# A layered graph network on one core: the low parts of x2 and x3 are formed on VectorE instead of GpSimd

## What is computed

```python
x = layernorm(x + L0(x))    # diffusion convolution with the adjacency
x = layernorm(x + L1(x))    # two dense layers with batch norm over all graphs: x2 needs all of them
x = layernorm(x + L2(x))    # two graph convolutions, then LSTMs over windows of 1, 2, 3 and 4 nodes
x = layernorm(x + L3(x))    # 8 Euler steps: h = h + dt*(alph*0.5*(adj@h - h) + h@w_eff - h + x0)
```

## Time and profile before

| what | value |
| --- | --- |
| median of 3 runs | 982.8 us (981.35 to 983.01) |
| the profiled execution | 981.68 us |
| its span | 979.6 us, so 2.1 us lie around the span |
| busy: PE, DVE, ACT, POOL | 915.4, 645.8, 576.6, 314.6 us |
| start stage, steps 0 and 1 | 206 to 424 us of the span |
| five middle steps | 424 to 849 us, 85.1 us each |
| step 7 and tail | 849 to 979.6 us |
| granted TensorE clock | 0.98 over the span, 1.00 in the middle steps |

### The profile page before, as it was taken

How to read it: one execution, slowest core, us unless ns; L and a number is a source line. 1 busy time by engine, 2 the same in 40 slices (tenths; PEclk the granted TensorE clock), 3 DMA queues, 4 the chain that set the end, 5 groups by cost and what they waited for, 6 DMA issues and landing times.

```text
span 979.6 us, 14819 instructions
## 1 busy us (share of the span) xinstructions
PE 915.4 (93%) x5115; PEld 792.3 (81%) x5115; DVE 645.8 (66%) x1576; ACT 576.6 (59%) x1292; POOL 314.6 (32%) x527
## 2 busy tenths in 40 slices
PE   8799998968899979999999999999999999999996
PEld 6688886346788658998998898899899889978986
DVE  5889995863467755666667666665766666675644
ACT  5467666823464556557737855774685576467352
POOL 2766555411101242035216304421620442150120
PEclk9999999989799989999999999999999999999999
DMA  5321201301011010101100110120011001000100
GB/s 177 119 75 57 74 33 46 122 27 65 0 33 55 1 33 1 54 2 44 56 11 11 33 66 1 44 65 1 12 33 66 1 22 44 1 12 1 33 22 22
DMA packets 26596, 38.56 MB, mean 39 GB/s; under 512 B 3333, under 2 KB 12422, under 8 KB 26010
## 3 DMA queue, kind: packets, MB, share of 16 engines
q1 hardware_dynamic: 26088, 36.05, 11.1%
q10 hardware_dynamic: 434, 1.57, 0.4%
HBM read 21.89 MB, written 15.73 MB: 38 GB/s over the span
## 4 chain that ended last, share of the span: by engine, by line
PE 55%; DVE 9%; POOL 7%; ACT 6%; issue 3%; ACTq 0%; POOLq 0%; DVEq 0%
PE psum L140 16%; PE psum L142 15%; PE psum L141 15%; PE psum L1811 2%; PE psum L1812 2%; PE psum L1815 2%; ACT gate L1378 1%; ACT x L1409 1%; POOL x_rstd L1311 1%; ACT raw L1474 1%; POOL out_rstd L1311 1%; POOL node_l L1329 1%; PE psum L1986 1%; DVE in_h L1543 1%; DVE shared L1617 1%
## 5 line engine op out<-in xcount | busy, mean ns | idle before, releaser
L1378 ACT ACTIVATE gate<-psum,gate_bias 128x256 f32<-128x256 f32 (+2 forms) x296 | 144.1, 559 | 85.2 <-PE psum L1815 62.4
L140 PE MATMUL psum<-in_h,wih_h 128*128 128x256 f32 (+2 forms) x312 | 107.3, 344 | 11.2 <-DVE in_l L1547 7.9
L142 PE MATMUL psum<-in_h,wih_l 128*128 128x256 f32 (+2 forms) x312 | 104.1, 334 | 0.0
L141 PE MATMUL psum<-in_l,wih_h 128*128 128x256 f32 (+2 forms) x312 | 103.6, 332 | 0.0
L1528 DVE TENSOR_TENSOR gate<-gate 128x256 f32<-128x256 f32 (+2 forms) x48 | 23.9, 499 | 88.9 <-ACT gate L1378 88.8
L140 PEld LDWEIGHTS psum<-in_h,wih_h 128*128 128x128 f32 x312 | 59.2, 190 | 22.9 <-DVE in_l L1547 11.6
L1345 POOL TENSOR_TENSOR gate<-in_h,in_l 128x512 f32<-128x512 f32 x14 | 17.9, 1303 | 164.7 <-DVE in_l L1547 164.7
L140 PE MATMUL psum<-e_h,shared 128*128 128x384 f32 x180 | 62.0, 345 | 5.5 <-DVE shared L1617 3.2
L1381 ACT ACTIVATE gate<-cell 128x512 f32<-128x512 f32 (+2 forms) x80 | 40.3, 503 | 42.6 <-DVE cell L1531 35.4
L141 PEld LDWEIGHTS psum<-in_l,wih_h 128*128 128x128 f32 x312 | 59.4, 190 | 5.1 <-issue 0.2
L142 PEld LDWEIGHTS psum<-in_h,wih_l 128*128 128x128 f32 x312 | 59.4, 190 | 4.7
(11 more groups left out here) (398 smaller groups left out, 2940.4 us busy)
## 6 DMA issues: line engine op xcount, KB each, us to landing
x_spill<-x SPq DMA_DIRECT2D x30, 256.0 KB, 2.0
xt<-in_x_t_dram SPq DMA_DIRECT2D x16, 256.0 KB, 2.7
raw<-x_spill SPq DMA_DIRECT2D x16, 256.0 KB, 3.0
o_spill<-xt SPq DMA_DIRECT2D x14, 256.0 KB, 2.0
xt<-o_spill SPq DMA_DIRECT2D x14, 256.0 KB, 3.2
x<-x_spill SPq DMA_DIRECT2D x14, 256.0 KB, 3.4
out_dram<-raw SPq DMA_DIRECT2D x14, 256.0 KB, 2.3
raw<-in_adj_t_dram ACTq DMA_DIRECT2D x1, 1024.0 KB, 8.8
```

What stands on the lines that cost most here:

```text
L140: pe.matmul(dst, lh, rh, start=start, stop=False, **kw)
L141: pe.matmul(dst, lh, rl, start=False, stop=False, **kw)
L142: return pe.matmul(dst, ll, rh, start=False, stop=stop, **kw)
L1378: nc.scalar.activation(gate[q][:, 0:n], banks[GATE_BANK[q]][:, 0:n], ACT.Tanh if q == 2 else ACT.Sigmoid, bias=gate_bias[:, p - 1, q:q + 1 ...
```

## The change

In all steps but the tail, POOL's pieces `norm` and `x3split` go away and DVE does the same subtraction: a new piece `x2low`, and the piece `x3low` that only the tail had. Each moved instruction is the same operation on the same 128x512 operands. 16 low parts of x2 and 14 of x3 move. ACT, PE and SP keep their order. Where the pieces stand in DVE's lists:

```diff
-        FILL_DVE = [[], ["ysum_1", "ysum_0", "turn_0"], ["x3t_0", "x3sum_1", "outsum"], ["power1_0", "power2_0", "gather0_0"],
-                    ["coefs0_0", "weight0_0"], ["turn_1", "coefs1_0"], ["gather1_0", "x3t_1"], ["power1_1", "weight1_0", "power2_1"],
+        FILL_DVE = [[], ["ysum_1", "ysum_0", "x3low_0", "turn_0"], ["x3t_0", "x3sum_1", "outsum", "x2low_0"], ["power1_0", "power2_0", "gather0_0"],
+                    ["coefs0_0", "weight0_0"], ["turn_1", "coefs1_0", "x3low_1"], ["gather1_0", "x3t_1", "x2low_1"], ["power1_1", "weight1_0", "power2_1"],
...
-        START_DVE = ["turn_0", "columns", "turn_1", "weff", "first_0", "first_1", "gather0_0", "gather0_1", "weight0_0", "weight0_1",
+        START_DVE = ["turn_0", "columns", "turn_1", "weff", "first_0", "x2low_0", "first_1", "x2low_1", "gather0_0", "gather0_1", "weight0_0", "weight0_1",
...
-        ONCE_DVE = [[], ["square", "twice", "turn_0"], ["first_3"], ["gather0_0", "cube", "second_0"],
-                    ["weight0_0", "fourth"], ["turn_1", "second_1", "fc_0"], ["gather1_0", "fc_1", "second_2"],
+        ONCE_DVE = [[], ["square", "twice", "turn_0"], ["first_3", "x2low_0"], ["gather0_0", "cube", "second_0"],
+                    ["weight0_0", "fourth"], ["turn_1", "second_1", "fc_0"], ["gather1_0", "fc_1", "second_2", "x2low_1"],
...
-        NEXT_DVE = [["addlate"], ["x3sum_0", "lift", "turn_0", "turn_vec"], ["mix_3", "x3sum_1", "mix_4"],
+        NEXT_DVE = [["addlate"], ["x3sum_0", "lift", "turn_0", "turn_vec"], ["x3low_0", "mix_3", "x3sum_1", "x2low_0", "mix_4"],
...
-                    ["lift_last", "weight0_0"], ["bias", "coefs0_0", "coefs1_0", "turn_1"]] + FILL_DVE[6:]
+                    ["lift_last", "weight0_0"], ["bias", "coefs0_0", "coefs1_0", "x3low_1", "turn_1"]] + FILL_DVE[6:]
...
-            def norm(g, j):
-                n = GB * g + j
-                pool.wait_ge(x2_hi, n + 1)
-                high, low = nodes(n)
-                nc.gpsimd.tensor_tensor(low[:], x2[j], f32(high[:]), ALU.subtract).then_inc(x2_lo, 1)
...
+            def x2low(g, j):
+                n = GB * g + j
+                dve.wait_ge(x2_hi, n + 1)
+                high, low = nodes(n)
+                nc.vector.tensor_tensor(low[:], x2[j], f32(high[:]), ALU.subtract).then_inc(x2_lo, 1)
```

More of the change, by code:

```diff
@@ L1146, in second_half @@
                     "coefs1", "inner", "innersum", "innerlow", "hlate", "addlate")
-        FRONT_NAMES = ("prep", "turn", "norm", "gather0", "gather1", "weight0", "weight1", "input")
+        FRONT_NAMES = ("x2low", "prep", "turn", "norm", "gather0", "gather1", "weight0", "weight1", "input")
         AHEAD_NAMES = ("ahead",)
@@ L1323, in turn @@
                 (power_of if g == 0 else root)(x2_norm[j], x2_asked, x2_shift, GB * g + j + 1)
-            def norm(g, j):
-                n = GB * g + j
-                pool.wait_ge(x2_hi, n + 1)
-                high, low = nodes(n)
-                nc.gpsimd.tensor_tensor(low[:], x2[j], f32(high[:]), ALU.subtract).then_inc(x2_lo, 1)
             def x3sum(g, j):
                 (power_of if g == G - 1 else root)(x3_norm[j], x3_asked, x3_shift, GB * g + j + 1)
-            def x3split(g, j):
-                n = GB * g + j
-                pool.wait_ge(x3_hi, n + 1)
-                high, low = x3_parts(g, j)
-                nc.gpsimd.tensor_tensor(low[:], x3[:, j, :, :], f32(high[:]), ALU.subtract).then_inc(x3_lo, 1)
             def whole_h(g):
@@ L1360, in split_e @@
                 nc.gpsimd.tensor_tensor(e_l[:], e[:], f32(e_h[:]), ALU.subtract).then_inc(constants_ready, 1)
-            run(None, {"split_e": split_e, "turn": turn, "norm": norm, "x3sum": x3sum, "x3first": lambda g: x3sum(g, 0), "x3early": x3sum, "x3split": x3split, "outsum": outsum,
+            run(None, {"split_e": split_e, "turn": turn, "x3sum": x3sum, "x3first": lambda g: x3sum(g, 0), "x3early": x3sum, "outsum": outsum,
                        "whole": whole_h, "clear": clear}, START_POOL, ONCE_POOL, NEXT_POOL, FILL_POOL, LAST_POOL, TAIL_POOL)
@@ L1778, in _ @@
                             "turn": turn, "weight0": weight0, "weight1": weight1, "x3sum": x3sum, "x3first": lambda g: x3sum(g, 0), "x3early": x3sum, "x3add": x3add,
-                            "addlate": x3add, "x3low": x3low, "outhalf": out_half,
+                            "addlate": x3add, "x2low": x2low, "x3low": x3low, "outhalf": out_half,
                             "x3t": x3t, "innersum": inner_sum, "innerlow": inner_low, "ysum": ysum, "outsum": outsum,
```

## The result

The changed kernel takes 975.51 us (median; 974.51 to 976.4) against 981.35 of the kernel before beside it: ratio 0.9937, 95% interval 0.9922 to 0.9953. Run twice more on other occasions it was at 977.51 (0.9961, 0.9945 to 0.9976) and 976.39 (0.9961, 0.9945 to 0.9976). So it is faster by 3.7 to 5.8 us. The prediction had 981.6, at least 979.6, and is wrong. Its forecast is measured from 982.8, the median of another occasion; the kernel before takes 980.3 to 981.5 in all the comparisons here.

A forecast was written before the change was run, and what follows sets the result against it. PE was taken to bound the kernel, busy 83.93 of 85.08 us in a middle step. Start -0.6, step 0 -0.4, step 1 +0.3 and middle steps -0.5 made -1.2 us, median 982.8 to 981.6, range 979.6 to 983.7.

The forecast's parts named there:

- Step 7 and tail ... 0: Step 7 has nothing behind x3low_0 and no node_l ahead of POOL's root, the tail is unchanged: 0.
- -0.1 a step, -0.5 in five: Middle steps: later turn_0 against earlier root of the last norm; five steps -0.5 us, bounds -2.0 and +1.0.
- D: Middle step: delay of ACT's L1409, waiting for POOL's root, as x3low_0 on DVE precedes turn_0; 0.7 us.
- The rule D - 0.79: Middle step: change in us per step, when PE starts coefs0 at 711.94 + D against 712.73.
- rival A: Middle steps: one more POOL root instruction ahead of L1536, D = 0.4, -0.4 a step, total -2.7, 980.1; chance 0.20.
- Start -0.6: Start stage: PE's first gather0 no longer waits for POOL's low part and starts 0.6 us earlier.
- step 0 -0.4: Step 0: DVE's product L1526 no longer overlaps POOL's low part, PE's wait for st_h goes; -0.4 us.
- Step 1 +0.3: Step 1: DVE's low part ahead of mix delays the chain PE waits for; +0.3 us, bounds 0 and +1.0.
- out follows the tanh: Middle step: out comes right after ACT's tanh, at 708.1 to 708.2 and not at 709.23.
- L1617's waits gone: Middle steps: PE's five waits of up to 0.6 us for DVE's L1617 disappear.
- in_l's wait about 1.0: Middle steps: PE's wait for DVE's in_l grows to about 1.0 us instead of 0.36.
- a sixth of 0.54: Whole kernel: share of the main forecast (chance 0.54) counted by scatter as faster by over 0.2%; with A 0.27.

The follow-up runs named there:

- c3: Also called x2 alone: against the kernel before, only x2's low parts moved to DVE, x3's left on POOL; 976.13 us, 0.9949.
- c8: Against the kernel before, only x2's low parts on DVE, and in step 1 x2low_0 placed behind mix_4; 977.32 us, 0.9959.
- c12: The kernel after with x3low_0 of the middle steps back on POOL, the other low parts on DVE; 974.81 us, 0.9935.
- c15: Same program as c12, timed again beside the kernel after: x3low_0 of the middle steps on POOL; 975.25 us, 0.9947.
- c13: The kernel before with ten unread 128x512 products put ahead of step 6's first cell; 981.25 us, 1.0000.
- c7: The change in the start, step 0 and step 1 alone, steps 2 to 7 as in the kernel before; 980.01 us, 0.9985.
- x3 alone: Against the kernel before, only x3's low parts moved to DVE, x2's left on POOL; 982.18 us, 1.0014.

## Why the prediction was wrong

- **"Step 7 and tail ... 0"** is the step that failed, and with it the first half, for which the sum has no term at all. By the order of the instructions both were right, but they took for granted that PE would run at the clock that it had. Step 7 lost 1.56 us since its 2.11 us wait, now 4.6 us earlier in the span and 2.1 nearer to the first full speed, was no longer followed by half speed. That this half speed comes and goes without an edit in step 7 is shown by c3 and c8, by c12 and c15, and by c13 in 11 executions. That it went here because the wait came earlier is the likely reading and is not shown.
- **The sum counted the first half as fixed.** It has the same instructions and took 2.69 less in the first comparison; steps 0 and 1 gave 0.55 of that back (-0.02 measured, where c7 puts the order's part at -0.57). Most of this is clock, too. A load that lands earlier gives 0.36 (PE's L796 starts at 3.50 instead of 3.86). TensorE first reaches full speed at 16.2 us before and at 13.7 after (there the 128x384 matmuls go from 0.52 to 0.34 us), an estimated 0.9. And the stretch from 180.0 to 183.5 has a granted clock of 0.51 before and full clock at the same place after, an estimated 1.5 to 1.6; the one stretch that after has instead, 37.5 to 41.2 with 0.54, costs about 0.1 by what is left of the sum. Over all seventeen profiles the half speed near 180 splits the first half in two: the eight that have it took 206.7 to 207.6, the nine others 204.5 to 205.8. All four with the old order up to step 5 are among the first, and all five with the order of after up to step 5 among the second; the others, with the same instructions there, fall on both sides. Why was not tested, and it stays open whether that belongs to a program or is chance.
- **Middle steps "-0.1 a step, -0.5 in five"**: mechanism right, size wrong. D came to 0.42 and not to 0.7. Measured -0.37 a step and -1.87 in five, so this term was 1.4 short. The rule D - 0.79 gave -0.79 and -0.37 where -0.84 (x2 alone, D = 0) and -0.37 (D = 0.42) were measured; x3 alone, which has D without the gain of 0.79, should give +0.42 and gave +0.54. The count of POOL's small instructions between DVE's products was one too slow: L1307 slipped in 0.04 us ahead of L1524 (I had 0.05, and put this case down as rival A with a chance of 0.20). The argument against it, that one which starts just ahead fares no better, was false: it took 0.22. With it L1310 lay beside the third product, and the power behind it took 1.04 instead of 1.49.
- **Start -0.6 and step 0 -0.4**: right. -0.61 in PE's wait for the low part, and -1.00 for both in c7.
- **Step 1 +0.3**: +0.43 in c7, of which 0.21 is there when PE's long wait ends. Right in sign and nearly in size.
- **"out follows the tanh", L1617's waits gone, in_l's wait about 1.0**: right, with 0.79 for the last, again by D.
- Rival A's D came true, but its 980.1 didn't. By the order alone the change is -0.57 - 1.87 = -2.4 us, within 0.3 of rival A; that the median lies so far below both is the clock. The other -3.6 of the profiled execution are step 7 with -1.56, and the first half, steps 0 and 1 and the tail with -2.0.
- In the chances, A (0.20) and a sixth of 0.54 make 0.29 for a gain of over 0.2%, not 0.27.

Of the three comparisons (-5.8, -3.7, -4.4), about 2.4 are order (1.9 of it shown by parts, the rest by one profile) and about 1.6 are the half speed in step 7. What is left, up to 1.8, is the clock of the first half and of step 1, which was seen and not controlled.

## What to carry to other kernels

Where TensorE sets the pace and stands still for some 2 us here and there, add to the sum a term of its own for half speed behind each such wait: 1.5 us here, either way, for an edit that only shifts the wait. Look in the profile before for a stage whose granted clock is below its neighbours' (0.98 against 1.00): it is a gain or a loss that a shift may bring. And when small dependent POOL instructions meet DVE products, price both cases of a near tie, since 0.05 us decides over 0.3.
